# Three phases of a transformer block woven into one program, with the first phase's instructions in another order

## The reference, cut to what matters

```python
x = x + attn_a(ln(x))   # 16 heads of 8, rotary with a radius per token, LN on q and k of each head,
                        # full softmax over the 256 tokens of a segment, output projection
x = x + ffn(ln(x))      # token shift, sigmoid(xr Wr) * (relu(xk Wk)^2 Wv)
x = x + attn_b(ln(x))   # below
x = x + ffn(ln(x))

def attn_b(x):          # 64 memory rows are put ahead of each segment
    out_swa = swa(x_in, wq, wk, wv, wo)          # 4 heads, window 64
    grads = grad(0.5 * sum((mlp(params, x_in) - out_swa) ** 2))   # over all 32 segments
    upd = (1 - alpha) * params - theta * grads
    out_mem = mlp(upd, x_in)
    return (sigmoid(out_swa @ lin1.T) * out_swa + sigmoid(out_mem @ lin2.T) * out_mem)[:, 64:]
```

## Time and profile before

| | us |
|---|---|
| median of 3 runs | 1560.99 |
| lowest and highest run | 1552.26, 1565.27 |
| the profiled execution | 1551.38 |
| its span, from the first to the last instruction | 1549.6 |
| PE, DVE, ACT, POOL busy | 1370.4, 1140.3, 915.5, 452.7 |
| first x load to last x2 of phase_a | about 0 to 716 |
| phase_b | about 720 to 1313 |
| phase_d | about 1323 to 1549 |

### The profile page before, as it was taken

How to read it: one execution, slowest core, us unless ns; L and a number is a source line. 1 busy time by engine, 2 the same in 40 slices (tenths; PEclk the granted TensorE clock), 3 DMA queues, 4 the chain that set the end, 5 groups by cost and what they waited for, 6 DMA issues and landing times. The chain is left out here.

```text
span 1549.6 us, 32924 instructions
## 1 busy us (share of the span) xinstructions
PE 1370.4 (88%) x10627; PEld 913.1 (59%) x10690; DVE 1140.3 (74%) x2898; ACT 915.5 (59%) x2490; POOL 452.7 (29%) x753
## 2 busy tenths in 40 slices
PE   4689999999999999883799999999999997699997
PEld 3345555555555555442566666666666664588886
DVE  5778888888888888732577777777777775378886
ACT  2267777777777777670456555555655552355553
POOL 4335545555555555321001000000100000133222
PEclk8689999999999999996899999999999999799998
DMA  2221222222222222202001000100100000332321
GB/s 70 67 68 53 72 70 75 74 74 74 75 67 75 75 75 71 66 10 62 17 22 32 22 22 22 32 22 22 32 21 22 22 21 21 87 87 84 86 83 39
DMA packets 103261, 80.89 MB, mean 52 GB/s; under 512 B 14436, under 2 KB 95780, under 8 KB 103092
## 3 DMA queue, kind: packets, MB, share of 16 engines
q1 hardware_dynamic: 102244, 78.63, 17.8%
q10 hardware_dynamic: 848, 0.15, 0.1%
HBM read 50.42 MB, written 28.31 MB: 51 GB/s over the span
## 5 line engine op out<-in xcount | busy, mean ns | idle before, releaser
L610 DVE TENSOR_REDUCE a_MX<-a_psS 128x4 f32<-128x1024 f32 x256 | 312.5, 1221 | 71.2 <-PE a_psS L244 71.2
L470 ACT ACTIVATE a_PT<-a_psE 128x512 f32<-128x512 f32 x512 | 278.2, 598 | 74.4 <-PE a_psE L257 71.0
L244 PE MATMUL a_psS<-a_KS,a_QS 48*128 48x256 f16 x1024 | 104.2, 283 | 52.9 <-DVE a_MX L610 37.0
L271 PE MATMUL a_psV<-a_PT,a_VX 128*32 128x256 f32 x2048 | 139.8, 391 | 0.5 <-ACT a_PT L470 0.5
L1437 POOL TENSOR_TENSOR b_SWB<-b_b2col,b_SW 128x128 f32<-128x128 f32 x65 | 26.3, 404 | 316.8 <-ACT b_SW L1188 316.8
L1216 ACT ACTIVATE b_HT<-b_psR 128x512 f32<-128x512 f32 x65 | 38.8, 597 | 121.0 <-PE b_psR L1070 121.0
L244 PEld LDWEIGHTS a_psS<-a_KS,a_QS 48*128 48x128 bf16 x1024 | 30.0, 95 | 135.8 <-DVE a_MX L610 62.5
L257 PE MATMUL a_psE<-a_QS,a_KS 50*128 50x256 bf16 x1024 | 100.0, 273 | 5.1 <-ACT a_PT L470 5.0
L1311 DVE SCALAR_TENSOR_TENSOR b_DZ<-b_U,b_psD 128x512 f32<-128x512 f32 x65 | 44.7, 688 | 80.7 <-PE b_psD L1032 79.1
L1222 ACT ACTIVATE b_PR<-b_psL,b_mx 128x128 f32<-128x128 f32 x260 | 92.4, 365 | 5.9 <-DVE b_mx L1335 5.9
L1057 PE MATMUL b_psL<-b_KT,b_QT 128*128 128x128 f32 x520 | 69.3, 277 | 23.4 <-issue 18.7
(11 more groups left out here) (275 smaller groups left out, 3461.6 us busy)
## 6 DMA issues: line engine op xcount, KB each, us to landing
a_KS<-kparts SPq DMA_DIRECT2D x64, 192.0 KB
a_QS<-qparts SPq DMA_DIRECT2D x128, 96.0 KB
qparts<-a_QP SPq DMA_DIRECT2D x64, 96.0 KB, 2.2
a_X<-x_in SPq DMA_DIRECT2D x32, 128.0 KB, 2.7
kparts<-a_KP SPq DMA_DIRECT2D x64, 64.0 KB, 2.1
x<-a_X SPq DMA_DIRECT2D x32, 128.0 KB, 2.1
b_X<-x SPq DMA_DIRECT2D x32, 128.0 KB, 2.3
zT<-b_XT SPq DMA_DIRECT2D x32, 128.0 KB, 1.7
```

Of the source, the lines that this page charges most:

```text
L244: mm = nc.tensor.matmul(psS[:, s, t, :], QS[rows, b % UK, p, t * P:(t + 1) * P], KS[rows, b % UK, p, :], start=True, stop=True)
L271: mm = nc.tensor.matmul(psV[32 * h:32 * h + 32, 0:T], VX[:, b % UV, kt, at:at + 32], PT[:, gg, kt, h, :], start=(gg == 0 and kt == 0), sto ...
L470: nc.scalar.activation(PT[:, g % 2, :, h + s, :], psE[s][:], ACT.Exp).then_inc(S["exp"], 1)
L610: nc.vector.reduce_max(MX[:, b % 2, :].rearrange("q (s n) -> q s n", s=2)[:, :, 2 * p:2 * p + 2], psS[:], AX.X).then_inc(S["max"], 1)
```

## The change

What it does:
- `build` makes one block. Each phase's engine function is now a generator that yields after every step, and `weave` advances them. Phase_b's constants are loaded two per step at steps 12 to 19 of phase_a. Folding stands behind step 34 on all engines. Behind step 36 come the clearing of most tiles and the x2 load of the first segment, and slots -4 and -3; behind step 37 slots -2 and -1. Phase_d's constants, its first loads and two memsets stand behind slot 20 of phase_b.
- Tiles and PSUM banks of phase_a are given back early, so that phase_b's lie over them; phase_b's fixed tiles (`fixed_b`) lie apart. Waits on phase_a's semaphores stand where something is overwritten. Phase_d uses semaphores of phase_a again and counts on from B (32).
- Phase_d reads ident and the updated weights from phase_b's tiles. The four stores and five loads go.
- In phase_a: SyncE's gather moves ahead of max_rows_in. On VectorE normalise moves up to between rsqrt 2 and 3, and rsqrt 5 goes behind the row maximum at p = 5. On GpSimd x2 moves ahead of qk_parts. The semaphores for x loads go from ten to four, with a wait on stats(b - 4) ahead of a load.

```diff
@@ phase_a, sync
+            wait(sp, "stats", b - 4, per=2 * NT)
...
             if on(c + 2):
                 load_next(c + 2)
+            if on(c - 1):
+                gather(c - 1)
             if on(c - 3):
                 max_rows_in(c - 3)
-            if on(c - 1):
-                gather(c - 1)
             if on(c):
                 parts(c)
@@ phase_a, vector
                     if on(c):
                         rsqrt(c, 2)
+                    if on(c - 5):
+                        normalise(c - 5)
+                    if on(c):
                         rsqrt(c, 3)
                 if p == 5:
                     if on(c):
+                        rsqrt(c, 5)
                         rsqrt(c, 6)
...
                         rsqrt(c, 4)
-                        rsqrt(c, 5)
-                    if on(c - 5):
-                        normalise(c - 5)
@@ phase_a, gpsimd
             if on(c):
                 x_bias(c)
-                qk_parts(c)
             if on(c - 6):
                 x2(c - 6)
+            if on(c):
+                qk_parts(c)
@@ phase_b, sync
-        for dst, src in CONSTS:
-            sp.dma_start(dst, src).then_inc(const_in, 16)
+        for part in range(PARTS):
+            for dst, src in CONSTS[2 * part:2 * part + 2]:
+                sp.dma_start(dst, src).then_inc(const_in, 16)
+            yield -8
...
+            sp.wait_ge(A["x2_out"][(b - 1) % 2], 16 * ((b - 1) // 2 + 1))
...
-        for b in (1,):
-            load(b)
-        steps(slot)
-
-        sp.wait_ge(S["upd"], 8)
-        for name, src in (("w1n", W1N[:]), ("w2tn", W2TN[:].rearrange("p c d -> p (c d)")), ("b1n", B1N[:]), ("b2n", B2N[:])):
-            sp.dma_start(dram[name], src).then_inc(fin_out, 16)
+        yield -6
+        load(1)
+        yield -5
+        yield from steps(slot)
@@ phase_b, tensor
+        yield from [-8] * PARTS
         pe.wait_ge(const_in, 16 * len(CONSTS))
         pe.wait_ge(S["wts"], 1)
         pe.wait_ge(S["folds"], 2)
+        pe.wait_ge(A["max"], NP * B)
...
         pe.wait_ge(S["folded"], 2)
+        yield -6
+        pe.wait_ge(A["exp"], 2 * NP * B)
+        yield -5
...
-        steps(slot)
-
+        yield from steps(slot)
+
+        pe.wait_ge(S["upd"], 1)
+        nc.tensor.matmul(psZ[:], fold[:], W1N[:], start=True, stop=True).then_inc(S["ends"], 1)
         wait_t(pe, "db1", TILES - 1)
...
-        nc.tensor.matmul(psZ[:], fold[:], W1N[:], start=True, stop=True).then_inc(S["upd"], 1)
@@ phase_b, vector
+        yield -6
+        dve.wait_ge(A["pv_ps"], NG * B)
+        nc.vector.memset(XT[:], 1.0).then_inc(S["zeros"], 1)
+        nc.vector.memset(XT0[:], 0.0).then_inc(S["zeros"], 1)
+        nc.vector.memset(V[:, 0, 0, :], 0.0).then_inc(S["zeros"], 1)
+        nc.vector.memset(QT[:], 0.0)
+        nc.vector.memset(wpm[:, PM:P], 0.0)
+        nc.vector.memset(wpm[:, 0:PM], float(B))
+        nc.vector.memset(E1[:], 0.0)
+        nc.vector.memset(DBZ[:], 0.0)
+        yield -5
...
+        for new, old in ((W1N, w1_t), (W2N, w2), (B1N, b1col), (B2N, b2col)):
+            nc.vector.tensor_scalar(new[:], old[:], keep[:], None, ALU.mult).then_inc(S["fin"], 1)
         wait_t(dve, "dw1_ps", TILES - 1)
...
+        dve.wait_ge(S["ends"], 2)
+        nc.vector.scalar_tensor_tensor(out=B1N[:], in0=psM[:, 0:NC], scalar=step_w[:], in1=B1N[:], op0=ALU.mult, op1=ALU.add).then_inc(S["upd"], 1)
+        nc.vector.tensor_copy(W1N[:], psZ[:]).then_inc(S["upd"], 1)
@@ phase_d
+    ident, w1n, w2tn, b1n, b2n = M["weights"]
...
+    def sync(sp):
+        sp.wait_ge(A["x2"], B)
+        for ring_of_a in A["x2_out"]:
+            sp.wait_ge(ring_of_a, 16 * (B // 2))
         for dst, src in CONSTS:
             sp.dma_start(dst, src).then_inc(const_in, 16)
...
+    def tensor(pe):
+        yield -1
+        pe.wait_ge(const_in, B + 16 * len(CONSTS))
+        pe.wait_ge(M["upd"], 4)
@@ build
+JOIN_B = {12: 1, 13: 1, 14: 1, 15: 1, 16: 1, 17: 1, 18: 1, 19: 1, 34: 1, 36: 3, 37: 2}
+JOIN_D = {20: 1}
+
+
+def weave(a, b, d):
+
+    for c in a:
+        for _ in range(JOIN_B.get(c, 0)):
+            next(b)
+    for s in b:
+        for _ in range(JOIN_D.get(s, 0)):
+            next(d)
+    for _ in d:
+        pass
```

More of the change, by code:

```diff
@@ L115, in steps @@
             body(c)
+            yield c
     def on(b):
@@ L216, in body @@
                 store(c - 6)
[L218 to L223, removed]
+        yield from steps(body)
+    def tensor(pe):
         def bias_columns():
@@ L451, in _, with scalar @@
         bias_columns()
-        steps(body)
-    @block.scalar
-    def _(act):
+        yield from steps(body)
+    def scalar(act):
         for dst, src in ACT_CONSTS:
@@ L574, in body, with vector @@
                         proj_v(c + 1)
-        steps(body)
-    @block.vector
-    def _(dve):
+        yield from steps(body)
+    def vector(dve):
         def clear_values(u):
@@ L758, in body, with gpsimd @@
                     clear_values(p)
-        steps(body)
-    @block.gpsimd
-    def _(pool):
+        yield from steps(body)
+    def gpsimd(pool):
         nc.gpsimd.memset(expo[:, 0:4], -0.5).then_inc(S["prep"], 1)
@@ L1441, in slot, with phase_d @@
                 nc.gpsimd.tensor_tensor(rs[:], rs[:], mhalf[:], ALU.pow).then_inc(S["rstd"], 1)
-        steps(slot)
-    return ctx
-def phase_d(nc, dram, B, held):
+        yield from steps(slot)
+    return ctx, dict(zt_out=zt_out, sw_out=sw_out, upd=S["upd"], weights=(ident, W1N, W2TN, B1N, B2N)), (sync, tensor, scalar, vector, gpsimd)
+def phase_d(nc, dram, B, A, M):
     ctx = ExitStack()
@@ L1553, in body, with tensor @@
                 load_z(c + 2)
-        steps(body)
+        yield from steps(body)
         for i in range(2):
-            sp.wait_ge(out_x[i], 16 * (B // 2))
-    @block.tensor
-    def _(pe):
-        pe.wait_ge(const_in, 16 * len(CONSTS))
+            sp.wait_ge(out_x[i], B + 16 * (B // 2))
+    def tensor(pe):
+        yield -1
+        pe.wait_ge(const_in, B + 16 * len(CONSTS))
+        pe.wait_ge(M["upd"], 4)
         def hidden(b, n):
@@ L1630, in body, with scalar @@
                 merge(c - 1)
-        steps(body)
-    @block.scalar
-    def _(act):
-        act.wait_ge(const_in, 16 * len(CONSTS))
-        act.wait_ge(S["init"], 1)
+        yield from steps(body)
+    def scalar(act):
+        yield -1
+        act.wait_ge(S["init"], B + 1)
+        act.wait_ge(M["upd"], 3)
         nc.scalar.preload_act_table_set("silu_and_others")
@@ L1681, in body, with vector @@
                     silu(c, n)
-        steps(body)
-    @block.vector
-    def _(dve):
+        yield from steps(body)
+    def vector(dve):
+        dve.wait_ge(A["x2"], B)
+        for ring_of_a in A["x2_out"]:
+            dve.wait_ge(ring_of_a, 16 * (B // 2))
         nc.vector.memset(mhalf[:], -0.5)
         nc.vector.memset(FZT[:], 0.0).then_inc(S["init"], 1)
-        dve.wait_ge(const_in, 16 * len(CONSTS))
-        dve.wait_ge(S["init"], 1)
+        yield -1
+        dve.wait_ge(const_in, B + 16 * len(CONSTS))
+        dve.wait_ge(S["init"], B + 1)
         def x3(b):
@@ L1752, in body, with gpsimd @@
                 shift(c - 2)
-        steps(body)
-    @block.gpsimd
-    def _(pool):
-        pool.wait_ge(S["init"], 1)
+        yield from steps(body)
+    def gpsimd(pool):
+        yield -1
+        pool.wait_ge(S["init"], B + 1)
         def body(c):
@@ L1771, in body @@
                 nc.gpsimd.tensor_tensor(DZ[:], FZT[:, 1:1 + T], FZT[:, 0:T], ALU.subtract).then_inc(S["dz"], 1)
-        steps(body)
-    return ctx
+        yield from steps(body)
+    return ctx, (sync, tensor, scalar, vector, gpsimd)
 def rotary_tables(tokens, dims):
```

207 lines of the change are left out of this document (113 added, 94 removed).

## The result

| | before | after |
|---|---|---|
| median of the runs (us) | 1557.87 (4 runs, 1552.26 to 1565.27) | 1498.99 (4 runs, 1496.58 to 1501.15) |
| ratio of times, 95% interval | | 0.9619 [0.9572, 0.9666] |
| profiled execution, its span | 1551.38, 1549.6 | 1496.58, 1494.8 |
| PE, DVE, ACT, POOL busy | 1370.4, 1140.3, 915.5, 452.7 | 1361.5, 1139.0, 913.8, 448.9 |

The changed kernel is 3.8% faster: 1499 us, where 1503 was forecast. The busy times are nearly those of before, so what went is idle and slow time. The runs also lie within 4.6 us of each other instead of 13.

The account below looks back on a forecast made before the run. Late gathers with slow TensorE stretches, VectorE's row-maximum stretch and idle program joins were taken as the limits: 1551.4 − 11 − 5.4 − 15 − 20 = 1500.0, plus 3 for the runs, 1503 us; range 1485 to 1522.

Parts of the forecast that it names:

- SyncE's order: First phase: gathers issued ahead of the maximum-row loads end most late-gather waits and slow stretches, saving 11 us.
- VectorE's order: First phase, fifth to sixth row maximum: moving rsqrt 5 and normalise saves 0.2 us per step, 5.4 us over 27.
- the 5 us that I let come back: First phase: ten late steps at 0.5 us, waiting for maximum rows now queued behind the gathers.
- The runs' excess: Median above profiled execution: 9.6 us before, put at 3 us after, since the change removes most gather lateness.
- GpSimd's order: First phase: x2 ahead of qk_parts delays the parts by about 0.75 us, hidden, costing nothing; 24 us without cover.
- First join: First to second phase: first z1 at 737.6 against 753.03; 15 us gained, bounds 10 and 22.
- the second term: First join: VectorE's memsets, 4.3 us, plus a statistics block, 1.2 us, delay the last fstats by 5.5 us.
- Second join: Second to third phase: first hidden product 18.8 us earlier and 1.5 us faster matmuls; 20 us, bounds 18 and 22.
- A: First phase: the gathers' wait only moves to the maximum rows; about 1517 us, chance 0.17.
- C: First phase, shifted product: maximum rows late every step, waits halving the clock; about 1576 us, chance 0.03.
- D: Joins gain little, 10 us each, with 10 from the first phase; 1521, or 1530 with runs' excess; chance 0.08.
- B: Joins near upper bounds, first phase gives all 16 and 8 us subtracted; 1485 us, chance 0.12.

Follow-up runs that it names:

- the three orders: Kernel before, still three programs, with the changed kernel's SyncE, VectorE and GpSimd orders together: 1533.97 us, ratio 0.9846.
- the late folding: Changed kernel with old VectorE order up to c = 5, memsets inside step 36, first x2 load earlier, folding behind step 36: 1489.47 us.

## Why the prediction was right, and where its steps were off

The time, its sign and the two joins held: 1499 measured, 1503 forecast. That the first phase's sum came out too is in part luck: SyncE's order gave 3.8 us more than forecast, and VectorE's order cost 3.5 us at the start that I had put at nothing. Step by step:

- **SyncE's order, 11 us (bounds 0 and 16).** Too small. It gave 13.3 us in the 27 steps, of which 1.3 in the last, and 1.5 us behind it (from the last first maximum to the last x1 52.82 us before, 51.30 with this order alone): 14.8 us in the profiles, of the 16 that I had counted in the same three places, near the upper bound. What failed is the 5 us that I let come back for late maximum rows: after the change TensorE waits for them once between 120 and 640 us (0.24 us, at 179.42, right behind a wait of 0.48 us for a gather). I had measured two loads of 8 KB by the 4.4 us that a gather of 96 KB took. The Trainium skill (DMA: Bandwidth & Descriptors, section Queues, rings and completion order) says that descriptors are consumed in ring order, and also that a later one may finish its write before an earlier one; that the moved load lands no earlier than the bulk of the gathers was my inference and not the page's. The trace agrees with the order in that the few waits stand right behind late gathers, and shows 0.24 us and not the low end of my range.
- **The runs' excess, 3 us instead of 9.6.** The median lies 2.4 us above the profiled execution (1498.99, 1496.58), but a profile is one draw: in the second set of the changed kernel it is 2.3 us above the median (1501.66, 1499.39). The cause held: SyncE's order alone saves 18.8 us by the medians, more than the 14.8 in the profiles, and narrows the runs from 18 us (1548.22 to 1566.16, one long run left aside) to 3.7. So the lateness of the gathers was also what made most of the difference between runs, as I had taken it. Together the first phase was to give 11 + 5.4 + 6.6 = 23 us against the median; the three orders gave 22.6.
- **VectorE's order, 5.4 us.** 5.3 us in the 27 steps, but by larger parts than I said: the fifth to the sixth maximum fell from 3.07 us in the steady step to 2.50, and the sixth to the seventh rose from 1.80 to 2.13, so the moved operation was not hidden by the idle 0.20 us. The 2.50 us also lie below the 2.6 to 2.9 that I had named as the sign. What failed here is the start, which I had put at nothing: 3.5 us lost where the same order lets the clock fall. With it the part is worth about 2 us net, and alone it gained nothing.
- **GpSimd's order, nothing.** Nothing else was seen, within some 5 us.
- **First join, 15 us.** It gave 20.4 - 4.5 = 15.9 (from the last x1 to the first z1, less the folding ahead of it). Of its terms: folding 4.5 predicted and 4.5 measured (+3.0 in the stretch, in which 1.5 us of the slow step of the earlier trace rows are gone; 55.81 - 51.30 against the kernel with SyncE's order alone); the clearing and the statistics ahead of the last fstats 5.5 and 5.7 (from the last x1 to it, 697.12 - 690.65 = 6.47 us, where it was 705.07 - 704.28 = 0.79); fstats to the end of the last x2 11.2 and 11.2 (708.34 - 697.12); the copies 0.9 and 0.9; scores to z1 10.4 and 9.8. That the sum came out hides a flaw in the second term: the clearing was not alone on the path. Taken away, it gave 1.2 us from x1 to fstats, and 4.4 only when the load under it went too.
- **Second join, 20 us.** 20.0 us to the first hidden product and 1.8 us for its full rate, 21.8 in all, inside the bounds of 18 and 22. The product starts 0.78 us behind the copy of W1N, within the 1 us that I had named. The reason I gave among the rivals, loads 45 slots ahead, is not one: they can be issued 13 us ahead for the same time.
- **Not in the sum:** the first row maximum came 1.5 us sooner, which is chance (42.66 in the second profile of the changed kernel, 40.85 in the first). The span ends 1.2 us slower after the last X4; that was not looked into.

Of the rivals, A (the wait moves to the maximum rows) is refuted by the kernel with SyncE's order alone, C and D by the result. B was nearer than the forecast for SyncE's order (16) and the second join (22), not for the rest. None of the signs of failure came: the tail of the first phase was stretched by 4.5 + 5.7 = 10.2 us, not by more than 15, the steady step is shorter, and the third phase waits for no load.

## What to carry to other kernels

Order a DMA queue by when data are needed, and put a load that must wait for a round trip behind those that needn't: six gathers held up behind two small loads cost 19 us here. A shortening elsewhere may pay only once such loads are in time (here 5.3 us in the steps with them in time, and no gain in the runs with them late), so test orders together and apart. Where two programs are joined, list everything that stands ahead of the one chain that crosses the join, per engine and per queue: taking away only the longest of them uncovers the next. And before two profiles are compared at one place, compare them at an earlier one: 2.7 of 5.0 us that looked like a gain of the late folding had been there 55 us before.

## What the runs showed of the hardware

- One operation of 0.23 us in another place of VectorE's order, and one step later the normalisation too, changed TensorE's granted clock twice between 94 and 122 us from 1.00 to 0.50, for some 3 and some 7 us, in each of seven profiles with that order at the start and in none of six without; together this cost 3.5 us. Idle stretches of 1.32 and 1.24 us in the same place were followed by a fall in one order and by none in the other.
- From the last first maximum to the last x1 the changed kernel took 55.81 us in its first profile, with the clock at 1.00 throughout, and 58.31 in its second, where the clock was at 0.50 for some 6 us. So two executions of one kernel can differ by 2.5 us in one place.
- SyncE's order took 12.5 us of waits for gathers out of the profile (13.8 to 1.3), and the runs gained 18.8 us; they had spread over 18 us before and over 3.7 after. That the other executions of the kernel before have more such waits than its profiled one, which is among its fastest, is likely but not shown.
- The third phase's constants and first tiles, issued at 1269.98 us and later, needed no more than 13 us of lead: the first product at 1282.81 waited for none of them.
